# Linear attention: the inverse of the floored denominators moves from VectorE to ScalarE

## What is computed

```python
q = (x @ Wq.T).reshape(Bx, Lx, NUM_HEADS, HEAD_DIM)
k = (x @ Wk.T).reshape(Bx, Lx, NUM_HEADS, HEAD_DIM)
v = (x @ Wv.T).reshape(Bx, Lx, NUM_HEADS, HEAD_DIM)
q = jax.nn.elu(q) + 1.0
k = jax.nn.elu(k) + 1.0
kv = jnp.einsum('blhd,blhe->blhde', k, v)
kv_cumsum = jnp.cumsum(kv, axis=1)
k_cumsum = jnp.cumsum(k, axis=1)
out = jnp.einsum('blhd,blhde->blhe', q, kv_cumsum)
denom = jnp.clip(jnp.einsum('blhd,blhd->blh', q, k_cumsum), 1e-06, None)
out = out / denom[..., None]
return out.reshape(Bx, Lx, HIDDEN) @ Wo.T
```

## Time and profile before

| | us |
|---|---|
| median of 3 runs | 2046.48 |
| the three runs | 2037.02, 2046.48, 2046.71 |
| the profiled execution | 2035.04 |
| its span (first to last instruction) | 2033.3 |
| its mean granted TensorE clock | 0.966 of full speed |

### The profile page before, as it was taken

One profiled execution on the slowest core, in us unless ns is written; L12 is line 12 of the kernel. 1 busy time (PEld: TensorE's weight loads), 2 busy tenths in 40 slices (PEclk: granted clock), 3 DMA queues, 4 the chain that ended last, 5 costly groups with the idle time before them and its releaser, 6 DMA issues. The chain is left out here.

```text
span 2033.3 us, 23699 instructions
## 1 busy us (share of the span) xinstructions
PE 1793.9 (88%) x7574; PEld 933.8 (46%) x7581; DVE 1527.7 (75%) x2505; ACT 869.3 (43%) x2055; POOL 704.0 (35%) x802
## 2 busy tenths in 40 slices
PE   5879998999998899889998999878887888789998
PEld 2336654555554565456655555422222323235555
DVE  5868875555555488656666887699999999988887
ACT  2225544555545454345554333544353543333332
POOL 3633222433333222312120000167677676550000
PEclk8989999999999899979998999989999999899999
DMA  6000000000000000010000000000000000000000
GB/s 239 1 0 0 1 0 1 1 1 1 1 1 1 1 1 1 0 43 1 1 2 1 1 0 1 11 5 7 10 0 16 0 16 1 0 1 0 0 1 21
DMA packets 9771, 19.94 MB, mean 10 GB/s; under 512 B 1072, under 2 KB 8368, under 8 KB 8752
## 3 DMA queue, kind: packets, MB, share of 16 engines
q1 hardware_dynamic: 9648, 18.42, 2.7%
HBM read 14.22 MB, written 1.05 MB: 8 GB/s over the span
## 5 line engine op out<-in xcount | busy, mean ns | idle before, releaser
L2046 POOL TENSOR_TENSOR ssm_hc<-ssm_h,ssm_cm 128x512 f32<-128x512 f32 x256 | 334.7, 1309 | 151.9 <-DVE ssm_h L2090 151.2
L2090 DVE TENSOR_TENSOR_SCAN ssm_h<-banks,ssm_dbx 128x512 f32<-128x512 f32 x256 | 309.6, 1210 | 2.3 <-DVE ssm_dbx L2082 2.3
L337 PE MATMUL banks<-ffn_x_high,up_high 128*128 128x512 f32 x544 | 286.2, 526 | 11.1 <-ACT ffn_s1g L872 9.6
L1992 PE MATMUL banks<-ssm_hc,const 128*128 128x512 f32 x512 | 270.4, 610 | 12.2 <-DVE ssm_gated L2067 9.3
L2030 ACT ACTIVATE banks<-banks,a_neg 128x510 f32<-128x510 f32 x256 | 167.1, 659 | 245.1 <-PE banks L1979 244.0
L338 PE MATMUL banks<-ffn_x_low,up_high 128*128 128x512 f32 x544 | 216.3, 398 | 0.0
L339 PE MATMUL banks<-ffn_x_high,up_low 128*128 128x512 f32 x544 | 215.5, 396 | 0.0
L1515 POOL TENSOR_SCALAR wide_pin<-wide_pin,wide_rden 128x256 f32<-128x256 f32 x256 | 117.6, 478 | 226.2 <-DVE wide_rden L1533 226.2
L373 POOL TENSOR_TENSOR x_norm<-x_centred,x_square 128x512 f32<-128x512 f32 x32 | 41.3, 1292 | 424.2 <-ACT x_square L368 424.2
L1710 ACT ACTIVATE ffn_th<-banks 128x512 f32<-128x512 f32 (+1 forms) x136 | 80.5, 597 | 241.1 <-PE banks L339 204.5
L2082 DVE TENSOR_TENSOR ssm_dbx<-banks,ssm_bm 128x512 f32<-128x512 f32 x256 | 170.9, 668 | 10.7 <-PE banks L1982 8.7
(11 more groups left out here) (227 smaller groups left out, 3387.6 us busy)
## 6 DMA issues: line engine op xcount, KB each, us to landing
ssm_packed<-ssm_parts SPq DMA_DIRECT2D x48, 64.0 KB, 2.0
up_whole<-in_up SPq DMA_DIRECT2D x1, 2304.0 KB, 15.2
weights<-in_weights SPq DMA_DIRECT2D x1, 2048.0 KB, 22.8
up_whole<-in_up SPq DMA_DIRECT2D x1, 2048.0 KB, 8.1
half<-in_half SPq DMA_DIRECT2D x1, 1440.0 KB, 18.2
weights<-in_weights SPq DMA_DIRECT2D x1, 1168.0 KB, 25.5
weights<-in_weights SPq DMA_DIRECT2D x1, 1152.0 KB, 8.2
const<-in_const SPq DMA_DIRECT2D x1, 1042.0 KB, 10.2
```

The costliest lines, as they stand in the source:

```text
L337: pe.matmul(out, w_high, x_high, start=True, stop=False)
L1992: pe.matmul(k.bank[5][:], k.c("hot")[:, P - row:2 * P - row], hc[:, i % HOLD, :], start=(i % NP == 0), stop=(i % NP == NP - 1)).then_inc(s ...
L2046: pool.tensor_tensor(hc[:, i % HOLD, :], h[:, i % HOLD, :], cm[:, i // NP % 2, :], ALU.mult) \
L2090: dve.tensor_tensor_scan(h[:, n % HOLD, :], k.bank[DELTA[n % AHEAD]][:], dbx[:, n % AHEAD, :], 0.0, ALU.mult, ALU.add).then_inc(s["h"], 1)
```

## The change

ScalarE works out the inverse of the floored denominators as exp(-ln(x)) in two instructions on the same tile `inv`. VectorE keeps the floor and loses the reciprocal and the wait before it. ScalarE's new function `invert` is called behind the pieces 0 to 2 of pass 0, and in the stage behind the three copies of each later pass. VectorE's floor gets a wait for the `qn` of the pass before, since it no longer writes `inv` behind its own last use of it. `Ln` and `Exp` use ScalarE's function table that is loaded at that time for the layer norm (`natural_log_exp_and_others`).

```diff
@@ -561,6 +561,14 @@
             act.wait_ge(s["k"], p + 1)
             link(act.activation(k_low[:], k.bank[4][:], ACT.Relu, scale=-1.0))
             act.activation(k_low[:], k_low[:], ACT.Exp, scale=-1.0).then_inc(s["k_low"], 1)
+        if n == 6:
+            invert(act, p)
+
+    def invert(act, p):
+        link = links.on(act)
+        act.wait_ge(s["floor"], p + 1)
+        link(act.activation(inv[:], inv[:], ACT.Ln))
+        act.activation(inv[:], inv[:], ACT.Exp, scale=-1.0).then_inc(s["inv"], 1)
 
     def gpsimd(pool, p, n):
 
@@ -593,9 +601,9 @@
                 .then_inc(s["ksum"], 1)
         if n == 6:
             dve.wait_ge(s["den"], p + 1)
+            if p >= 1:
+                dve.wait_ge(s["qn"], p)
             dve.tensor_scalar(inv[:], k.bank[5][:], 1e-6, None, ALU.max).then_inc(s["floor"], 1)
-            dve.wait_ge(s["floor"], p + 1)
-            dve.reciprocal(inv[:], inv[:]).then_inc(s["inv"], 1)
 
     def run(nxt):
         kv, state = sb("lin_kv", [P, 2, T]), sb("lin_state", [P, 2, T])
@@ -658,6 +666,7 @@
                     scalar(act, p, n)
                 for cols in cuts[3 * p - 3:3 * p]:
                     act.activation(k.up_high[0][:, cols], k.up_whole[0][:, cols], ACT.Copy).then_inc(s["up_high"], 1)
+                scalar(act, p, 6)
             follow.rest()
```

## The result

| | before | after |
|---|---|---|
| median, us | 2037.35 (6 runs, 2034.16 to 2046.71) | 2021.90 (6 runs, 2021.14 to 2023.63) |
| ratio | | 0.9915, 95% interval 0.989 to 0.994 |
| profiled execution, us | 2035.04 | 2021.40 |
| its span, us | 2033.3 | 2019.6 |
| its mean granted clock | 0.966 | 0.968 |

The kernel is 0.85% faster (0.6 to 1.1%) by the ratio, which follows the means of the runs; it is 13.64 us faster between the two profiled executions and 15.45 (0.76%) between the medians. The forecast was 2032.0 us, from the median 2046.48 of the three runs shown; with three more runs that median is 2037.35. The spread of before has to be known for this: its runs fall into two groups. Of 86 runs of it on record 52 lie between 2034 and 2039.2 us and 34 between 2041 and 2046.7. Two of the three shown were of the upper one; they are the longest of all 86, 2.2 us above the next.

A forecast was written before the change was run, and what follows sets the result against it. VectorE was taken as nearest to a bound, its reciprocal on the pacing path. Terms 2.05 + 9.90 + 3.15 - 0.6 = 14.5 us, off the median 2046.48, gave 2032.0 us; range 2021 to 2041.

The forecast's parts named there:

- the base: Whole kernel: the 14.5 us gain was taken off 2046.48 us, the median of three timed runs, giving 2032.0 us.
- B: Rival: TensorE's slow-clock stretches stay or come elsewhere in the stage; gain 11.35 us, 2035.1 us; chance 0.19.
- C: Rival: GpSimd becomes the pace, gaining only 2.09 us per handover; gain 8.3 us, 2038.2 us; chance 0.14.
- D: Rival: later stages hand the gain back through one more stretch at TensorE's lower clock; 2041.7 us; chance 0.15.
- E: Rival: slower, three more 20 us stretches at half speed in later stages cost 28 us; 2060 us; chance 0.05.
- The pair on ScalarE: Ln and Exp, 0.63 us each, give the inverse 1.33 us after the floor; pass 0 gains 2.05 us.
- ScalarE's cover: ScalarE delays nothing: the wait for the floor falls into its 14.31 us idle hole before the next layer norm.
- The early clock of pass 0: Pass 0's groups start earlier on a TensorE still at 1.2 GHz: 0.6 us lost, between 0 and 2.05.
- 3.30 us at each handover: Passes 1 to 3: VectorE's floor-to-product step falls from 3.97 to 0.67 us; three times 3.30 gives 9.90 us.
- GpSimd's half microsecond to spare: Running sums behind the floor: GpSimd's weightings end in time, so VectorE keeps 3.30 us with half a microsecond spare.
- The clock: Both TensorE clock sags behind handovers, 1.58 us each, go with the 2.75 us idle gaps: 3.15 us gained.
- VectorE beside GpSimd: VectorE's product beside GpSimd's `qn` could slow by 0.4 us three times; cost set at 0, 1.2 us kept for the range.

The follow-up runs named there:

- experiment 3: Changed kernel plus an unread VectorE reciprocal just behind each floor, the early inverse kept: 2037.02 us against 2037.82 for the kernel before, ratio 0.9994.
- 1 and 2: Kernel before with inverses moved to ScalarE only in pass 0 (first: 2036.04 us, ratio 0.9994) or only in passes 1 to 3 (second: 2025.17 us, 0.9937).
- experiment 4: Kernel before plus 10 unread matmuls on TensorE in each of the three idle stretches of 2.75 us: 2033.36 us against 2037.82, ratio 0.998.
- 7 and 8: Changed kernel plus four unread matmuls behind each of three floors (first: 2025.39 us), or with the floor moved to ScalarE too (second: 2028.19 us).
- 5: Changed kernel plus two unread activations ahead of Ln in each inverse, which comes 1.3 us later: 2026.18 us against 2037.33 before, ratio 0.9942.

## Why the prediction was right or wrong

**The mechanism was right, and its parts in the right order of size.** VectorE's occupancy at the handovers was the path (experiment 3), the three of them carry the gain (1 and 2), and the two slow stretches of TensorE were worth 1.58 and 1.53 us and went when the idle stretch was filled (4). The sum was 14.5 us; the stage gained 13.93, and 13.09 when both kernels were run again. That 13.93 is so near to 14.5 is in part luck: the first step of before came out 1.6 us apart in its two profiled executions.

**The step that failed is the base**: "I put the change on the median: 2046.48 - 14.5 = 2032.0". The sum against the profiled execution gave 2020.5, and the profiled execution after is 2021.4. The three runs shown could not tell that 2046 was the upper of two groups, but 2037.02 and 2035.04 beside it were a warning that I read as a scatter around the median. With the median of six runs, 2037.35, the same sum would have been 2022.9, 1.0 us from the result. Set against that median, 2032.0 is a gain of 5.4 us where 15.45 were measured. The range carried the same error: 2021 to 2041 reaches 9 us above the forecast, and the result lies at its lower end, inside only because that end was taken from the profiled execution and not from the median. B, C, D and E were counted from 2046.48 too, so their times are some 9 us too high against the median of six runs.

Point by point:

- *The pair on ScalarE*: 630 ns for Ln and for Exp, at the lower end; `qn` 2.09 us behind the floor in pass 0, so 2.07 gained for 2.05. No overlap of the two, as the second waits for the first; the 93 ns of the Trainium skill ("ScalarE: Activation LUTs", section on what a table load costs) don't show in this pair: Ln starts at 69.74 and Exp 0.66 us later. Where the next one doesn't read what the one ahead wrote, the trace agrees with the page: L562 starts at 82.21, 0.10 us before L560 ends (81.68 + 0.63).
- *ScalarE's cover*: it held. It waits 6.43 us for the floor, and 3.47 for the next layer norm after the pair.
- *The early clock of pass 0*: 0.6 us set against the gain, 0.79 came out (2.07 - 1.28). It varies: the first step was 24.93 us when the changed kernel was run again, and 27.31 instead of 25.72 when before was. So the runs can't tell 0.6 from a value some tenths above or below it.
- *3.30 us at each handover*: 3.11. The step from floor to product shrank by 3.39 (the prediction left 0.67 for the floor; it is 0.58 to the next start), and 0.27 is given back before the addition to x, which comes 5.75 us behind that product instead of 5.48. I said that VectorE keeps all of it and looked for the next limit in GpSimd. It is TensorE (7 and 8), whose pairs follow each other there without idle time; VectorE is some 0.2 us ahead of it.
- *GpSimd's half microsecond to spare*: right, by 0.76 us lost per handover when the inverse came 1.3 us later (5).
- *The clock*, 3.15 us: right in size for the pair of executions compared. That both sags go was an assumption; it held in all nine profiled executions of kernels without VectorE's reciprocal at the handovers, none of which has a slow pair behind one, and experiment 4 shows the idle stretch as the cause: with it filled and nothing else changed, the slow pairs are gone in its profiled execution, and seven of its ten runs are shorter than any of the 25 beside them. How many there are before is not fixed: the second time one stood at a handover and 1.6 us lay in the first step.
- *VectorE beside GpSimd*: 0 set, right; the 1.2 us of the upper bound did not come. The product behind the floor (L706) takes 0.68 us beside GpSimd. Before it took 0.63 there, but 0.68 at 84.60 too, with GpSimd idle from 82.98 to 87.14, so the 0.05 isn't GpSimd's. The rule of the Trainium skill ("GPSIMD Engine Reference", key points), which names VectorE instructions with two SBUF inputs, fits: this one reads one operand from PSUM. L383, with two, takes 1.08 us beside GpSimd, 1.09 before.
- *The rivals*: B, C and E did not come. D's mechanism, long runs through the later stages' clock, is there, but in both kernels. I gave it a sign against the change, and the 12 runs of the changed kernel, one of them long, give none.

## What to carry to other kernels

An in-line instruction of 3.35 us on the engine that paced this loop cost 3.1 us each time, and at two of three places 1.6 us of the neighbour's clock besides. Look first for an idle engine in that hole (ScalarE stood still for 14 us), and price the handover by the step between the instructions around it, not by the busy time. After the engine is freed, look for the next limit among those that run back to back there, not at the one that had waited longest, and test each by giving it a little more or less work: here two of them were busy throughout, and only one set the pace. And before a change is put on a base, ask whether the runs shown form one group or two: a sum made against one execution belongs to that execution's group.

## What was not expected of the hardware

The fall of the granted clock to the lower level was tied to TensorE's idle stretch of 2.75 us, but not to each. With all three filled none came (experiment 4). With three open, two came in one execution of the kernel before (behind the first and the third) and one in another (behind the third); one came in the kernel with the change in pass 0 alone (behind the second) and one with VectorE's extra reciprocal (behind the first). In the kernel with four matmuls more, pairs of 1.9 to 2.05 us appeared at 110 us, behind no handover, where the others had none. What decides between them no run here shows. Also left open is why some runs of the kernel before have a mean granted clock of 0.962 to 0.964 and others mostly 0.966 to 0.968 (three of 48 have 0.964); the medians of the two groups are 2043.1 and 2036.6 us.
